# A gated two-layer block: the first attention's scores as three single-pass products of rounded parts and remainders, instead of one float32 product

## The reference

```python
def _L0_xattn_ref(query, key, value, mask, Wq, Wk, Wv, Wo):   # b=8, t=128, 512 columns
    h, kv_h, d = 32, 8, 128
    g = h // kv_h
    q = apply_rope((query @ Wq).reshape(b, t, h, d))
    k = apply_rope((key @ Wk).reshape(b, t, kv_h, d))
    v = (value @ Wv).reshape(b, t, kv_h, d)
    logits = einsum('btkgd,bTkd->bkgtT', q.reshape(b, t, kv_h, g, d), k) * 0.0883883
    logits = 30 * tanh(logits / 30)
    weights = softmax(where(mask, logits, -1e30))
    attn = einsum('bkgtT,bTkd->btkgd', weights, v).reshape(b, t, h * d)
    return attn @ Wo

x = x + tanh(g_xattn[0]) * _L0_xattn_ref(layernorm(x), ctx, ctx, mask, Wq, Wk, Wv, Wo)
x = x + tanh(g_ffn[0])   * _L0_ffn_ref(layernorm(x), ...)     # low-rank experts, untouched
x = x + tanh(g_xattn[1]) * _L1_xattn_ref(layernorm(x), ...)   # second attention, untouched
x = x + tanh(g_ffn[1])   * _L1_ffn_ref(layernorm(x), ...)     # top-2 experts, untouched
```

## Time and profile before

| | us |
|---|---|
| device time, median of 3 runs | 925.3 (923.52 to 929.58) |
| device time of the profiled execution | 922.56 |
| its span (first to last instruction) | 920.7 |
| around the span | 1.86 |
| TensorE busy | 863.2 (94%) |
| VectorE busy | 603.6 (66%) |
| ScalarE busy | 326.8 (35%) |
| GpSimd busy | 417.0 (45%) |

### The profile page before, as it was taken

The page is one execution under the profiler, slowest core; times in us unless marked ns, Lnnn a source line. Parts: engine busy times, 40 slices in busy tenths (PEclk is TensorE's granted clock), DMA queues, the critical chain, the costliest instruction groups (busy, mean ns, idle before and its releaser), DMA issues.

```text
span 920.7 us, 13835 instructions
## 1 busy us (share of the span) xinstructions
PE 863.2 (94%) x4747; PEld 705.9 (77%) x4747; DVE 603.6 (66%) x1062; ACT 326.8 (35%) x590; POOL 417.0 (45%) x423
## 2 busy tenths in 40 slices
PE   4999999999999999999999999999999998849992
PEld 4778878977877787887897787787799997437782
DVE  5975675366576537567537657768898887676345
ACT  4424124214214213313321411423366677533230
POOL 4652353153162224144216315334989775527651
PEclk9999999999999999999999999999999999959997
DMA  9020120011111002012001100212264321753448
GB/s 324 17 92 1 35 92 1 12 46 47 35 46 46 14 1 92 1 35 91 1 12 46 46 1 15 68 40 85 64 168 122 80 59 39 291 185 111 162 154 317
DMA packets 42320, 71.16 MB, mean 77 GB/s; under 512 B 7049, under 2 KB 14794, under 8 KB 42066
## 3 DMA queue, kind: packets, MB, share of 16 engines
q1 hardware_dynamic: 37138, 58.00, 19.8%
q0 software_dynamic: 3680, 12.06, 3.9%
q10 hardware_dynamic: 1440, 0.24, 0.1%
HBM read 53.64 MB, written 10.22 MB: 69 GB/s over the span
## 4 chain that ended last, share of the span: by engine, by line
PE 85%; DVE 6%; issue 2%; POOL 2%; DMA 2%; ACT 1%; SPq 1%; ACTq 1%; DVEq 0%
PE ps L1418 18%; PE ps L1420 18%; PE ps L1419 18%; PE ps L1539 6%; PE ps L1531 6%; PE ps L1668 5%; PE ps L1547 3%; PE ps L1656 3%; PE ps L1649 2%; PE ps L1782 1%; POOL w_lo L518 1%; DVE h L953 1%; PE ps L1639 1%; POOL y_rows L670 1%; DVE stats L947 1%
## 5 line engine op out<-in xcount | busy, mean ns | idle before, releaser
L544 POOL TENSOR_TENSOR q_t<-rot_a,rot_b 128x512 f32<-128x512 f32 x64 | 82.7, 1292 | 151.1 <-DVE rot_b L998 151.1
L996 DVE TENSOR_TENSOR rot_a<-ps,cos 128x512 f32<-128x512 f32 x80 | 55.1, 689 | 85.7 <-PE ps L1420 85.0
L1418 PE MATMUL ps<-xt_hi,wq_hi 128*128 128x512 f32 x256 | 107.6, 420 | 0.6 <-DVE rot_b L998 0.6
L1418 PE MATMUL ps<-wo_hi,at_hi 128*128 128x512 f32 x256 | 106.7, 417 | 0.4 <-DVE at_lo L1106 0.4
L1420 PE MATMUL ps<-xt_hi,wq_lo 128*128 128x512 f32 x256 | 101.1, 395 | 0.0
L1419 PE MATMUL ps<-xt_lo,wq_hi 128*128 128x512 f32 x256 | 101.0, 394 | 0.0
L778 ACT ACTIVATE ps<-ps 128x512 f32<-128x512 f32 x64 | 37.2, 581 | 178.6 <-PE ps L1531 178.6
L1420 PE MATMUL ps<-wo_hi,at_lo 128*128 128x512 f32 x256 | 100.2, 391 | 0.0
L1419 PE MATMUL ps<-wo_lo,at_hi 128*128 128x512 f32 x256 | 99.8, 390 | 0.0
L791 ACT ACTIVATE at_hi<-ps 128x512 fp32r<-128x512 f32 x64 | 38.3, 598 | 171.5 <-PE ps L1547 171.5
L1111 DVE TENSOR_TENSOR X<-ps,X 128x512 f32<-128x512 f32 x64 | 44.2, 690 | 74.4 <-PE ps L1420 74.1
(11 more groups left out here) (223 smaller groups left out, 2081.1 us busy)
## 6 DMA issues: line engine op xcount, KB each, us to landing
wq_raw<-in_wq SPq DMA_DIRECT2D x8, 1024.0 KB, 5.3
wo_raw<-in_wo SPq DMA_DIRECT2D x8, 1024.0 KB, 5.1
w_raw<-in_we SPq DMA_DIRECT2D x8, 1024.0 KB, 6.8
X<-in_x SPq DMA_DIRECT2D x4, 512.0 KB, 12.6
wk_raw<-in_wk SPq DMA_DIRECT2D x8, 256.0 KB, 2.8
q_t<-in_ctx_t SPq DMA_DIRECT2D x2, 1024.0 KB, 9.8
wv_raw<-in_wv SPq DMA_DIRECT2D x4, 512.0 KB, 4.3
ctx_s<-in_ctx SPq DMA_DIRECT2D x8, 256.0 KB, 3.0
```

The source lines that it names most:

```text
L544: nc.gpsimd.tensor_tensor(dst, rot_a[:, r % 2, :], rot_b[:, r % 2, :], ALU.add).then_inc(rope_ok, 1)
L996: nc.vector.tensor_tensor(heads(rot_a[:, r % 2, :]), heads(bank), bcast(cos[:, :], 4), ALU.mult)
L1418: nc.tensor.matmul(dst, w_hi, x_hi, start=start and k == 0, stop=False)
```

## The change

The scores become three products of rounded parts and remainders, by the same `product`. After each `rope_sum` ScalarE rounds the tile (`turned_hi`, counted by `sh_ok`) and VectorE takes the remainder (`turned_lo`, counted by `sl_ok`); `scores` waits for `sl_ok` where it waited for `rope_ok`. There are ten such tiles in a group, 80 in all, 128x512 each. VectorE takes the remainder of a tile behind the `rotate` of the next one. To have room in SBUF for `q_hi` and `k_hi`, the remainder `q_lo` is written over `q_t`, `k_lo` over `k_t`, and `wo_lo` over `wo_raw`. With the last of these, `load_wo(g)` has to wait for `wo_mm`, all output products of the group before, and stands behind `load_wq(g)` in SyncE's queue; the waits of ScalarE's `wo_split` are as they were. `v_ones` loses two unused columns.

```diff
-        wo_raw = sb("wo_raw", [P, G, D])
         wo_hi = sb("wo_hi", [P, G, D], F32R)
+        wo_raw = over("wo_raw", [P, G, D])
         wo_lo = sb("wo_lo", [P, G, D], F32R)
-        q_t = sb("q_t", [P, G, N])
-        k_t = sb("k_t", [P, N])
-        v_ones = sb("v_ones", [P, B, 2, P + 4])
+        q_hi = sb("q_hi", [P, G, N], F32R)
+        q_t = over("q_t", [P, G, N])
+        q_lo = sb("q_lo", [P, G, N], F32R)
+        k_hi = sb("k_hi", [P, N], F32R)
+        k_t = over("k_t", [P, N])
+        k_lo = sb("k_lo", [P, N], F32R)
+        v_ones = sb("v_ones", [P, B, 2, P + 2])
...
+        def turned_tile(r, queries, keys):
+
+            if r < 2:
+                return keys[:, r * HALF:(r + 1) * HALF]
+            half, head = divmod(r - 2, G)
+            return queries[:, head, half * HALF:(half + 1) * HALF]
...
@@ SyncE, for g in range(1, KV)
-                sp.wait_ge(wo_lo_ok, CREDIT + G * g)
-                load_wo(g)
                 sp.wait_ge(qp_mm, CREDIT + 8 * g)
                 load_wq(g)
+                sp.wait_ge(wo_mm, CREDIT + B * g)
+                load_wo(g)
...
@@ ScalarE
+            def turned_hi(g, r):
+                ac.wait_ge(rope_ok, CREDIT + 10 * g + r + 1)
+                hi_part(turned_tile(r, q_hi, k_hi), turned_tile(r, q_t, k_t), sh_ok)
...
+            turned_hi(0, 0)
+            turned_hi(0, 1)
...
+                for r in range(2, 7):
+                    turned_hi(g, r)
                 weights(0)
                 weights(1)
+                turned_hi(g, 7)
                 for b in range(B):
                     if b + 2 < B:
                         weights(b + 2)
+                    if b < 2:
+                        turned_hi(g, 8 + b)
...
+                if not last:
+                    turned_hi(g + 1, 0)
+                    turned_hi(g + 1, 1)
...
@@ VectorE
+            def turned_lo(g, r):
+                ve.wait_ge(sh_ok, CREDIT + 10 * g + r + 1)
+                nc.vector.tensor_tensor(turned_tile(r, q_lo, k_lo), turned_tile(r, q_t, k_t), turned_tile(r, q_hi, k_hi).bitcast(F32),
+                                        ALU.subtract).then_inc(sl_ok, 1)
...
             turned_first(6)
             turned_first(7)
+            turned_lo(0, 0)
+            turned_lo(0, 1)
...
-                for r in range(2, 8):
+                rotate(g, 2)
+                for r in range(3, 8):
                     rotate(g, r)
+                    turned_lo(g, r - 1)
                 mask(0)
                 mask(1)
+                turned_lo(g, 7)
                 rotate(g, 8)
                 scale(0)
                 mask(2)
+                turned_lo(g, 8)
                 lo_of(0)
                 rotate(g, 9)
                 for b in range(1, B):
                     scale(b)
                     if b + 2 < B:
                         mask(b + 2)
+                    if b == 1:
+                        turned_lo(g, 9)
                     if last and b >= B - 2:
                         mix_lo(b - B + 2, b - B + 2)
                     add(b - 1)
...
                 add(B - 1)
+                if not last:
+                    turned_lo(g + 1, 0)
+                    turned_lo(g + 1, 1)
...
@@ TensorE
                 def scores(b):
                     if b in (0, 4):
-                        pe.wait_ge(rope_ok, CREDIT + 10 * g + 6 + b)
+                        pe.wait_ge(sl_ok, CREDIT + 10 * g + 6 + b)
                     pe.wait_ge(e_ok, CREDIT + B * g + b - 1)
-                    nc.tensor.matmul(ps[:, 2 + b % 2, :], k_t[:, b * P:(b + 1) * P], q_t[:, :, b * P:(b + 1) * P],
-                                     start=True, stop=True).then_inc(s_mm, 1)
+                    rows = slice(b * P, (b + 1) * P)
+                    product(ps[:, 2 + b % 2, :], [(k_hi[:, rows], k_lo[:, rows], q_hi[:, :, rows], q_lo[:, :, rows])]).then_inc(s_mm, 1)
```

More of the change, by code:

```diff
@@ L287, in flamingo_gated_two_layers @@
         kp_mm, vp_mm, qp_mm, rot_ok, rope_ok, v_ok = sem("kp_mm"), sem("vp_mm"), sem("qp_mm"), sem("rot_ok"), sem("rope_ok"), sem("v_ok")
+        sh_ok, sl_ok = sem("sh_ok"), sem("sl_ok")
         s_mm, th_ok, ex_ok, e_ok = sem("s_mm"), sem("th_ok"), sem("ex_ok"), sem("e_ok")
@@ L538, in rope_sum @@
                 gp.wait_ge(rot_ok, CREDIT + 10 * g + r + 1)
-                if r < 2:
-                    dst = k_t[:, r * HALF:(r + 1) * HALF]
-                else:
-                    half, head = divmod(r - 2, G)
-                    dst = q_t[:, head, half * HALF:(half + 1) * HALF]
-                nc.gpsimd.tensor_tensor(dst, rot_a[:, r % 2, :], rot_b[:, r % 2, :], ALU.add).then_inc(rope_ok, 1)
+                nc.gpsimd.tensor_tensor(turned_tile(r, q_t, k_t), rot_a[:, r % 2, :], rot_b[:, r % 2, :], ALU.add).then_inc(rope_ok, 1)
             def group(g, p, odd, last=False):
@@ L701, in _ @@
                 ac.dma_start(dst, src).then_inc(consts_in, 16)
-            start_counts(ac, (ot_ev, gates_ok, hth_ok, cth_ok, wkh_ok, wvh_ok, wqh_ok, wo_hi_ok, v_ok, th_ok, ex_ok, ah_ok, wbh_ok,
+            start_counts(ac, (sh_ok, ot_ev, gates_ok, hth_ok, cth_ok, wkh_ok, wvh_ok, wqh_ok, wo_hi_ok, v_ok, th_ok, ex_ok, ah_ok, wbh_ok,
                               lge_ok, zt_ok, qkh_ok, p_ok, pt_ok, gelu_ok, weh_ok, r_ok, gh_ok, tri_ok))
@@ L939, in _ @@
         def _(ve):
-            start_counts(ve, (wo1_ok, ctl_ok, prep_v, cap_ok, stat_ok, aggr_ok, h_ok, htl_ok, rot_ok, e_ok, rec_ok, at_ok, al_ok,
+            start_counts(ve, (sl_ok, wo1_ok, ctl_ok, prep_v, cap_ok, stat_ok, aggr_ok, h_ok, htl_ok, rot_ok, e_ok, rec_ok, at_ok, al_ok,
                               x1_ok, bbg_ok, lg_ok, lgm_ok, lgs_ok, lgi_ok, al2_ok, zw_ok, tb_ok, hc_ok, keep_ok, pen_ok, qk_ev,
```

## The result

The changed kernel takes 950.5 us (median of 4 runs, 948.24 to 955.15); the kernel before takes 924.9 beside it (4 runs). The ratio is 1.0285, with a 95% interval of 1.0248 to 1.0322. The profiled execution has a span of 946.4 us against 920.7: 25.7 us more, where the prediction's sum had 23.1.

What follows compares the result with a forecast made beforehand. TensorE's queue was taken to bound the kernel, with hand-over slack deciding: -10.9 + 7.2 + 5.6 + 3.2 + 16.8 + 1.2 = +23.1 us on 922.56, 945.7; with runs' median 2.7 higher, forecast 948 us, range 931 to 956.

Steps and rivals of the forecast that it cites:

- TensorE is the bound and nothing may be late: Whole kernel: TensorE, busy 94% of the span, bounds it; the slack of each hand-over to it decides.
- Saving, -10.9: TensorE's scores: 0.86 us becomes three products, 0.69; 0.17 saved on each of 64 scores, -10.9 us.
- The tile phase, +0.9 and +0.8 in odd groups: Before `scores(0)`: 0.9 us in 8 groups, +7.2; at query tile 4: 0.8 in four odd groups, +3.2.
- The output weights' load, +5.6: Value tile 2 waits behind the later load: 2.6 us in groups 2 and 6, 0.4 in group 4.
- The batch phase, +16.8: Attention batches: remainders 8 and 9 delay four hand-overs, 0.4 + 0.2 + 1.0 + 0.5 us in each of 8 groups.
- `scores(4)` and `output(1)`: Batch phase: remainder 9 makes `scores(4)` wait 1.0 us and `output(1)` 0.5 more, per group.
- `output(0)` and `turn(1)`: Batch phase: remainder 8 ahead of `lo_of(0)` makes `output(0)` wait 0.4 us and `turn(1)` 0.2, per group.
- The start, +1.2: Start of group 0: two key remainders stand in front of `rotate(0, 2)`, for which TensorE already waited; +1.2 us.
- C: Rival, all remainders: existing gaps hold them before TensorE asks; 921 us, or 915 with the load hidden too; chance 0.10.
- B: Rival, VectorE and GpSimd: no mutual waiting that matters; waits +19.6 less 10.9, 934 us; chance 0.17.
- D: Rival, score products: no cheaper than before, the moving operand being read in four pieces; 957 us; chance 0.08.
- A: Rival, VectorE and GpSimd: the lock holds to each instruction's very end, 4 us more in all, 952; chance 0.2.

Runs made afterwards that it cites:

- the products alone: Kernel before with scores as three single-pass products of rounded parts, no remainders of queries and keys, no ScalarE rounding of them: 917.3 us, ratio 0.9898.
- the hand-over gone: Kernel before with three-product scores, no query or key remainders, and output products needing the context's remainder placed last: 908.4 us, ratio 0.9813.
- the PSUM operand: Changed kernel with the second operand of `turned_lo` read from a PSUM bank instead of SBUF (wrong data): 941.2 us, ratio 1.0167 to the kernel before.
- early load: Changed kernel with `wo_raw` over `e_w` and `attn`, so the output weights load after the previous group's last `turn`: 938.8 us, ratio 1.0138 to the kernel before.
- the kernel before with the late load: Kernel before with only the output weights' load moved behind the query weights' load, waiting for the last output product: 932.8 us, ratio 1.0087.
- both together: Changed kernel with `turned_lo` reading a PSUM operand and the output weights loaded early: 929.6 us, ratio 1.0057 to the kernel before.

## Why the prediction was right

**TensorE is the bound and nothing may be late: shown.** All 25.9 us came in the first attention, and in the stretch of the earlier trace rows TensorE went from 100.00 to 95.70 us busy out of 100.

**Saving, -10.9: the step that was mis-sized.** The size of one score was right (three products at the 0.23 of the earlier trace rows; 0.47 for three scores in the products alone, 0.18 at best in a batch with the hand-over gone). The sentence that "a score shorter by 0.17 still fits" in later batches was wrong. The earlier trace rows with the earlier trace rows seemed to leave 0.4 us between the end of `lo_of` and the output product. But with the scores shortened by 0.17 the batch got only 0.08 shorter, and 0.02 to 0.05 in the changed kernel, so at most 0.1 of it was free. The weight load had been released by `at_lo` already; I had read the time between its start and the product's as slack. In the kernel with the products alone 6.0 us were saved instead of 10.9.

**The tile phase, +0.9 and +0.8 in odd groups: right.** 1.7 predicted, 1.85 measured (18.65 less 16.80). That the two engines wait for each other was shown twice, by the ends of the records and by the PSUM operand, which gave 0.93 of it back. The early load gave 0.97 back. By the distances between tile starts, 0.89 of this is the wait of query tile 4 with what hung on it, and 0.07 belongs to `scores(0)`; in the even groups, where tile 4 doesn't wait, the first column is 0.97 longer. So the two terms are separate, as the walk had them: 0.9 for `scores(0)` and 0.8 for tile 4 worked out, 0.9 to 1.0 and 0.9 measured.

**The output weights' load, +5.6: right in groups 2 and 6, wrong in group 4.** The idle records show 2.59 and 2.37 us there. By the distance from `turn(7)` to the first query tile behind it (20.36, 20.15, 20.15 us after, 17.44, 20.04, 17.44 before) the values cost 2.9, 0.1 and 2.7 in groups 2, 4 and 6, where 2.6, 0.4 and 2.6 were worked out. (0.08 of each belongs to the next keys: with the early load, and no wait, the distance is 17.52.) In group 4 I let the issue gap of 1.91 cover all but 0.4. The gap did not come in this kernel, and TensorE waited 2.38 for `v_ones` in its place. From load to load the group is 2.0 longer, as by the terms.

**The batch phase, +16.8: right where the long path is, too much ahead of it.** `scores(4)` and `output(1)`, 1.5 less one score's 0.17: 1.33 predicted and 1.30 measured. `output(0)` and `turn(1)`, 0.6 less 0.17: 0.43 predicted, 0 measured. Remainder 8 cost nothing: it fell into the 1.96 us in which VectorE had been idle in front of `lo_of(0)`, and `lo_of(0)` began 1.35 us behind `turn(0)`, where it had begun 1.34 behind it before. So `scale(1)` was no later either. The saving of `scores(3)` was lost in front of `turn(1)`, whose weight load starts 0.05 behind the end of `attn` as in the kernel before, and no more:

```profile
291.16 0.68 DVE L1134 TENSOR_TENSOR at_lo<-ps,at_hi 128x512 fp32r<-128x512 f32 x1
294.09 0.69 DVE L1128 TENSOR_TENSOR attn<-ps,denom_inv 128x512 f32<-128x512 f32 x1
294.83 0.42 PEld L1584 LDWEIGHTS ps<-ident,attn 128*128 128x128 f32 x4 [0.30 <-DVE attn L1128]
```

**The start, +1.2: somewhat more.** The wait for query tile 2 went from 0.55 to 1.98, +1.4. Up to the first load of query weights the kernel is 2.1 later, where the terms give 1.2 + 0.9 - 0.5 = 1.6.

**The sum.** By the measured columns an odd group has +1.85 - 0.40 + 1.30 - 0.02 - 0.05 = +2.7 up to `turn(4)`, of the 2.8 that the loads show, where the terms gave 2.4. Even groups got 4.9, 2.0 and 4.5 longer, against 4.2, 2.0 and 4.2. And so 23.1 became 25.7. That it came so near is in part luck, since errors cancel. In a group 0.52 of the saving behind `scores(0)` did not come (0.11 in the second column, 0.41 in the three from `turn(2)` on), and 0.17 came in the products of the next keys, where no term stood; against it `output(0)` and `turn(1)` cost 0.43 less than was worked out. Over eight groups that is +4.2, +1.4 and -3.4.

**The rivals.** C (the gaps hold everything) fails at the place that it named: `scores(4)` waits 0.66. B and D are refuted by the PSUM operand and by the products alone. A, the lock held to the very end, would have given 952, which is not far from the result. But the ends of the records show 0.13 to 0.16 us in all five cases worked out above and 0.13 to 0.15 in all 81 of the first attention, so its nearness is no evidence for it.

**What stays open.** That the first column is still 0.28 above 16.80 with both the exclusion and the late load gone is what the walk of rival B gave for the remainders' place in the queues (0.3); no run takes this place away alone. Why the stretch of the next keys got 0.17 longer was not found. Nor was why the issue gap at the loop's second turn comes in some kernels and not in others: 1.91, 1.96 and 2.29 us in the three that have the float32 scores, none in the eight with three products.

## What to carry to other kernels

Where the bounding engine is 100% busy, read a saving on it against the next hand-over. Look at when the weight load in front of the product starts and when the operand that released it was ready. If it starts right behind (0.05 to 0.06 us here), a part of the saving or all of it is lost there, and an order that puts the late operand last can give it back. An added operation costs by how late it makes the next engine, not by how busy its own engine is. VectorE at 54 of 100 us was not the trouble, and a remainder that fell into its idle time cost nothing. The trouble was an operation of 0.6 between a product and its reader, above all one with two SBUF operands beside a busy GpSimd. Move such operations behind the ones somebody waits for before giving the change up: the same products went from +2.9% to -0.8% by order and placement alone.

## What the runs showed of the hardware

- TensorE's granted clock can halve around a single wait. In the first attention the eleven traces have four stretches at 1.2 GHz, and each begins at the end of a wait or gap of 1.96 to 2.61 us or at most 1.6 us behind it. Waits or gaps of 1.9 to 2.6 us in front of value tiles were followed by such a stretch in 4 of 11 cases (two of three in the PSUM operand kernel, two of three in the kernel before with the late load, none of three after the change, none in the single gaps of the two others). The wait of 1.97 to 2.00 us at the start of group 0, in six kernels, was not followed by one. Each stretch cost 1.2 to 1.5 us. The waits were of the same length in both kinds (2.50 with, 2.59 without), so the length alone does not decide; what does was not found.
- The stretch behind the first attention, the same code in all, took 309.2 us (after) to 315.4 (both together), though nothing there was edited. In part this is the clock: from 640 to 700 us it was granted at 1.00 in the kernels before and after, and at 0.94 in that one. Read an effect of a few us at the end of the stretch that was edited, not at the end of the span.
- VectorE and GpSimd with SBUF operands on both sides wait for each other in both directions, if VectorE's operation reads two operands from SBUF: 0.69 became up to 1.82 on VectorE (median 0.79), 1.30 became up to 1.80 on GpSimd (median 1.73). Counted back by its own length, each got going 0.13 to 0.16 us before the other's record ended. With one of VectorE's operands in PSUM the 64 records of each kind were at their own length (at most 0.69 and 1.31).
